# Feed-forward on one core: gate and up as one row of 1408 columns over three PSUM banks

## The reference, cut to what matters

```python
BLOCK = 16
def fp4_quant_dequant(x):                      # last dim in blocks of 16
    xb = x.reshape(shape[:-1] + (shape[-1] // BLOCK, BLOCK))
    scale = jnp.max(jnp.abs(xb), axis=-1, keepdims=True) / 6.0
    scale = jnp.maximum(scale, jnp.float32(1e-12))
    xn = xb / scale
    idx = jnp.searchsorted(_MID, jnp.abs(xn))
    q = _GRID[idx] * jnp.sign(xn) * scale
    return q.reshape(shape)

def fp4_linear(x, w):
    return jnp.einsum('bsk,nk->bsn', fp4_quant_dequant(x), fp4_quant_dequant(w))

gate = fp4_linear(x, w_gate)                   # 256 -> 704
y = fp4_linear(x, w_up)                        # 256 -> 704
h = jax.nn.silu(gate) * y
return fp4_linear(h, w_down)                   # 704 -> 256
...
x = x + _L0_attn_a_ref(_layernorm(x), ...)
x = x + _L0_ffn_ref(_layernorm(x), w_gate, w_up, w_down)
x = x + _L0_attn_b_ref(_layernorm(x), ...)
x = x + _L0_ffn_ref(_layernorm(x), w_gate, w_up, w_down)
```

## Time and profile before

| | |
|---|---|
| median of 3 runs | 3568.77 us (3567.9 to 3569.11) |
| span of the profiled execution, first to last instruction | 3544.7 us |
| PE busy | 3052.4 us, 86% of the span |
| DVE busy | 2796.0 us, 79% |
| ACT busy | 2188.0 us, 62% |
| POOL busy | 1119.2 us, 32% |

### The profile page before, as it was taken

One profiled execution on the slowest core, in us unless ns is written; L12 is line 12 of the kernel. 1 busy time (PEld: TensorE's weight loads), 2 busy tenths in 40 slices (PEclk: granted clock), 3 DMA queues, 4 the chain that ended last, 5 costly groups with the idle time before them and its releaser, 6 DMA issues. The chain is left out here.

```text
span 3544.7 us, 69866 instructions
## 1 busy us (share of the span) xinstructions
PE 3052.4 (86%) x23640; PEld 2351.6 (66%) x23640; DVE 2796.0 (79%) x7241; ACT 2188.0 (62%) x5392; POOL 1119.2 (32%) x665
## 2 busy tenths in 40 slices
PE   5898888988886999995888888888888886799998
PEld 3666666666655888884555556556555554788888
DVE  4777777767767999992788888888888886799997
ACT  3777777777762434441777878777777785344443
POOL 1000000000004555553124444433333343455554
PEclk9999999999996999997899989999999997899999
DMA  5354453534422000001344444344434443111000
GB/s 91 51 75 65 61 76 50 75 65 62 72 37 106 13 19 19 19 19 30 48 63 69 64 73 69 60 63 70 66 60 70 68 61 83 42 37 34 28 31 25
DMA packets 134180, 193.96 MB, mean 55 GB/s; under 512 B 15126, under 2 KB 81558, under 8 KB 133142
## 3 DMA queue, kind: packets, MB, share of 16 engines
q1 hardware_dynamic: 133830, 189.49, 31.3%
HBM read 45.65 MB, written 28.84 MB: 21 GB/s over the span
## 5 line engine op out<-in xcount | busy, mean ns | idle before, releaser
L436 ACT ACTIVATE a_probs<-a_probs,a_negmax 128x176 f32<-128x176 f32 (+4 forms) x1024 | 502.4, 491 | 261.0 <-DVE a_negmax L355 257.2
L355 DVE CUSTOM_DVE_ANT_0 a_probs<-a_mask,a_score 128x176 f32<-128x176 f32 (+4 forms) x1024 | 403.6, 399 | 254.5 <-PE a_score L511 116.6
L520 PE MATMUL a_turned<-ident,a_probs 128*128 128x128 f32 (+1 forms) x2176 | 405.2, 280 | 60.3 <-DVE a_pT L364 32.8
L1752 DVE CUSTOM_DVE_ANT_0 b_u<-b_u,b_score 128x512 f32<-128x512 f32 x512 | 340.3, 680 | 129.7 <-PE b_score L2007 128.3
L1877 ACT ACTIVATE b_u<-b_u,b_negmax 128x512 f32<-128x512 f32 x512 | 367.1, 717 | 107.0 <-DVE b_negmax L1752 105.4
L1281 PE MATMUL f_y_bank<-f_wdT,f_hqT 128*128 128x256 f32 x1536 | 357.0, 382 | 40.7 <-ACT f_hqT L1220 37.7
L1744 DVE SCALAR_TENSOR_TENSOR b_u<-b_u,b_score 128x1024 f32<-128x1024 f32 x256 | 309.6, 1214 | 92.1 <-ACT b_u L1870 89.6
L1870 ACT ACTIVATE b_u<-b_score 128x1024 f32<-128x1024 f32 x256 | 262.2, 1025 | 159.8 <-PE b_score L1997 159.3
L1281 PEld LDWEIGHTS f_y_bank<-f_wdT,f_hqT 128*128 128x128 f32 x1536 | 284.6, 190 | 89.6 <-issue 56.5
L2016 PE MATMUL b_turned<-ident,b_u 128*128 128x128 f32 x2048 | 318.1, 280 | 24.1 <-DVE b_pT L1758 18.9
L520 PEld LDWEIGHTS a_turned<-ident,a_probs 128*128 128x128 f32 (+1 forms) x2176 | 237.3, 134 | 136.1 <-ACT a_probs L436 61.5
(11 more groups left out here) (237 smaller groups left out, 7037.0 us busy)
## 6 DMA issues: line engine op xcount, KB each, us to landing
b_stack<-b_part SPq DMA_DIRECT2D x192, 256.0 KB, 8.1
a_stack_q<-a_part SPq DMA_DIRECT2D x192, 128.0 KB, 4.5
a_wide_k<-a_part SPq DMA_DIRECT2D x96, 164.0 KB, 7.8
a_stack_k<-a_part SPq DMA_DIRECT2D x96, 128.0 KB, 4.6
xs<-in_x_dram SPq DMA_DIRECT2D x16, 512.0 KB, 10.6
x_before_b<-xs SPq DMA_DIRECT2D x16, 512.0 KB, 2.9
b_xin<-x_before_b SPq DMA_DIRECT2D x16, 512.0 KB, 12.3
b_xres<-x_before_b SPq DMA_DIRECT2D x16, 512.0 KB, 3.8
```

Source lines behind the costliest of these rows:

```text
L355: dve.tensor_tensor_reduce(out=probs[:, n % 2, j, 0:keys(n)], in0=mask_of(n), in1=score[j][:, 0:keys(n)], scale=-1.0, scalar=3.0e38, op0=A ...
L436: act.activation(probs[:, n % 2, j, 0:keys(n)], probs[:, n % 2, j, 0:keys(n)], ACT.Exp, bias=negmax[:, n, j:j + 1], scale=-1.0, accum_out= ...
L520: m = nc.tensor.transpose(turned[j % 2][0:rows, u, :], chunk(n, probs[:, n % 2, j, :], u), ident[:])
L1752: dve.tensor_tensor_reduce(out=u[:, n, j, :], in0=u[:, n, j, :], in1=score[:, j, :], scale=-0.05, scalar=3.0e38, op0=ALU.add, op1=ALU.min, ...
```

## The change

Gate and up get one tensor of three banks, gate_up, in place of two of two banks each. The weights of both already stand side by side as 1408 columns; they are now cut at the banks' borders into 512, 512 and 384 columns in place of four pieces of 352. Each piece is still six products, so a tile has 18 in place of 24. Gate is columns 0 to 703, up is 704 to 1407: bank 1 holds the end of gate and the beginning of up. s_gate is raised by the last product of bank 1, s_up by that of bank 2. Bank 0 waits for the silu of the tile before, banks 1 and 2 wait for its f_hid. The bank that comes free holds the block maxima (`amax`, two tiles of 44 columns), which lay in SBUF; in the profile of the changed kernel they have the name f_scaled.

```diff
-        amax = sb("amax", [P, 2, NB])
...
-        gate = pb("gate", [P, 2, SEQ])
-        up = pb("up", [P, 2, SEQ])
+        gate_up = pb("gate_up", [P, 3 * SEQ])
         xT_bank = pb("xT_bank", [P, SEQ])
         hT_bank = pb("hT_bank", [P, 2 * SEQ])
+        scaled = pb("scaled", [P, SEQ])
         y_bank = pb("y_bank", [P, SEQ])
+        amax = [scaled[:, i * NB:(i + 1) * NB] for i in range(2)]
...
                 dve.wait_ge(s_silu, T + 1)
                 dve.wait_ge(s_up, T + 1)
-                dve.tensor_tensor(out=hid[:, i, :].rearrange("p (a b) -> p a b", a=2),
-                                  in0=silu[:, i, :].rearrange("p (a b) -> p a b", a=2),
-                                  in1=up[:, :, both], op=ALU.mult).then_inc(s_hid, 1)
+                dve.tensor_tensor(out=hid[:, i, :], in0=silu[:, i, :], in1=gate_up[:, INNER:2 * INNER],
+                                  op=ALU.mult).then_inc(s_hid, 1)
                 dve.wait_ge(s_hid, T + 1)
-                dve.tensor_reduce(out=amax[:, i, :], in_=blocks(hid[:, i, :]), axis=AX.X, op=ALU.max,
+                dve.tensor_reduce(out=amax[i], in_=blocks(hid[:, i, :]), axis=AX.X, op=ALU.max,
                                   apply_absolute_value=True).then_inc(s_h, 1)
                 dve.wait_ge(s_h, 2 * T + 1)
-                dve.tensor_scalar(out=nscale[:, t, :], in0=amax[:, i, :], scalar1=-SIXTH, scalar2=-SCALE_MIN,
+                dve.tensor_scalar(out=nscale[:, t, :], in0=amax[i], scalar1=-SIXTH, scalar2=-SCALE_MIN,
                                   op0=ALU.mult, op1=ALU.min)
-                dve.tensor_scalar(out=amax[:, i, :], in0=amax[:, i, :], scalar1=SIXTH * TIE_DOWN, scalar2=SCALE_MIN,
+                dve.tensor_scalar(out=amax[i], in0=amax[i], scalar1=SIXTH * TIE_DOWN, scalar2=SCALE_MIN,
                                   op0=ALU.mult, op1=ALU.max).then_inc(s_h, 1)
                 dve.wait_ge(s_h, 2 * T + 2)
-                dve.reciprocal(out=inv[:, i, :], in_=amax[:, i, :]).then_inc(s_inv, 1)
+                dve.reciprocal(out=inv[:, i, :], in_=amax[i]).then_inc(s_inv, 1)
...
                 act.wait_ge(s_gate, T + 1)
-                act.activation(silu[:, t % 2, :].rearrange("p (a b) -> p a b", a=2), gate[:, :, 0:HALF],
-                               ACT.Silu).then_inc(s_silu, 1)
+                act.activation(silu[:, t % 2, :], gate_up[:, 0:INNER], ACT.Silu).then_inc(s_silu, 1)
...
-            def expand(s, t, which):
+            def expand(s, t, bank):
+
                 T = tile(s, t)
-                if which == 0:
+                if bank == 0:
                     pe.wait_ge(s_xTm, 4 * s + t + 1)
-                free = (s_silu, s_hid)[which]
-                wait(pe, free, T)
-                dst = (gate, up)[which]
-                for a in range(2):
-                    at = which * INNER + a * HALF
-                    products = [(k, i, j) for k in range(KC) for i, j in ((0, 0), (0, 1), (1, 0))]
-                    for p, (k, i, j) in enumerate(products):
-                        m = mm(dst[:, a, 0:HALF], xqT[:, i, k, t * P:(t + 1) * P], wguT[:, j, k, at:at + HALF],
-                               start=p == 0, stop=p == len(products) - 1)
-                m.then_inc((s_gate, s_up)[which], 1)
+                wait(pe, (s_silu, s_hid, s_hid)[bank], T)
+                at = slice(bank * SEQ, min((bank + 1) * SEQ, 2 * INNER))
+                products = [(k, i, j) for k in range(KC) for i, j in ((0, 0), (0, 1), (1, 0))]
+                for p, (k, i, j) in enumerate(products):
+                    m = mm(gate_up[:, at], xqT[:, i, k, t * P:(t + 1) * P], wguT[:, j, k, at],
+                           start=p == 0, stop=p == len(products) - 1)
+                if bank:
+                    m.then_inc((s_gate, s_up)[bank - 1], 1)
...
                     if t is not None:
                         expand(s, t, 1)
+                        expand(s, t, 2)
                     if behind(3):
                         down(*behind(3))
```

More of the change, by code:

```diff
@@ L975, in ffn @@
     NB = INNER // BLOCK
-    HALF = INNER // 2
     LAG = 3
@@ L1133, in hidden @@
                 T, i = tile(s, t), t % 2
-                both = slice(0, HALF)
                 if not isinstance(T, int) or T >= 2:
```

## The result

| | before | after |
|---|---|---|
| median, same chip | 3568.94 us (3567.9 to 3569.12, 4 runs) | 3609.06 us (3608.42 to 3615.59, 4 runs) |
| ratio, 95% interval | | 1.0126 (1.0112 to 1.0140) |
| span of the profiled execution | 3544.7 us | 3607.3 us |

The account below looks back on a forecast made before the run. DVE's chain bounds the kernel (31.15 us per four tiles), TensorE close behind; at 8.09 us per tile, two stages add 42 us: span 3544.7 to 3587, plus 24.1 around it, gives 3610 us, range 3570 to 3635.

Parts of the forecast that it names:

- The chain bank 1, silu, move, down product: TensorE and ScalarE: 1.87 us needed against bank 2's 1.05, so a 0.82 us wait before every down product.
- Fewer products: TensorE's gate and up: 18 products in place of 24 save 0.02 us per tile, range 0 to 0.12.
- The period: Feed-forward time per tile: 7.29 + 0.82 - 0.02 = 8.09 us.
- f_nscale: DVE scaling of 44 columns: PSUM input cuts 0.84 to about 0.17 us; net gain for the kernel taken as 0.
- f_hid at even distances: Sign in the profile after: f_hid, gate times up, stands 8.1 us apart in all four slots.
- the part on bank 1: Bank 1's wait for the previous tile's f_hid stays hidden; cover gone only if DVE fell 4.6 us behind.
- the three signs of being wrong: f_y_bank waiting under 0.5 us, f_hid at unequal distances again, or the 18 products clearly under 3.9 us.
- What lies around the span: Time outside the profiled span: 3568.77 - 3544.7 = 24.1 us, added to the forecast span of 3587.
- The range: Forecast's own range 3592 to 3628 us; widened to 3570 to 3635 to hold 8 in 10.
- The faster rival: ScalarE's move arrives in time, DVE sets 29.8 us per sequence: -40 us, 3529; needs wait below 0.50 us; chance 0.15.
- The draw: Wait before the down product is 0.45 to 0.55 us, giving 3562 to 3575 us; chance 0.05.
- the slower rival: Dear PSUM operations on DVE or a falling granted clock add 15 to 30 us: 3625 to 3640; chance 0.05.

Follow-up runs that it names:

- the move first: Changed kernel with ScalarE's move of f_hT_bank to f_hqT (tile T-3) put before the silu of tile T; 3526.69 us, ratio to before 0.9901.
- transposes between: Changed kernel with TensorE's six transposes of f_hq put between bank 1 and bank 2, ScalarE's order kept; 3537.17 us, ratio to before 0.9945.
- Both magnitudes swapped: Changed kernel with move before silu and, in slot 0, magnitude of h before that of x; profiled twice; 3505.75 us, again 3503.92 us.

## Why the prediction was right, point by point

- *The chain bank 1, silu, move, down product:* shown. Taken away it gives 85 us back (the move first), covered by other work it gives 72 (transposes between), lengthened by 0.65 us it costs 78, and put into the old kernel it costs 66 to 69. The wait was forecast at 0.82 us by start times; it is 3.33 less 2.53 of products, 0.80. The profile counts 127 such waits in the 128 tiles of both stages and shows it here as 0.64, since it counts from the products' modelled end.
- *Fewer products:* 0.02 us was forecast. It is nothing: where TensorE does not wait (the timeline under "Both magnitudes swapped"), bank 0 takes 1.47 us and banks 1 and 2 take 2.53, 4.00 us as in the earlier trace rows. The cost went with the 8448 columns. The other end, 0.12 us, is excluded, and so is a period under 8 us.
- *The period:* 8.17 for 8.09 us. Two terms were mis-sized: the 0.02 above, and a down product that follows a wait takes 2.66 us, not 2.59. The earlier trace rows had that in them (in the same timeline the next instruction starts 2.67 us later), and I had read the 2.59 from a product without a wait. The 120 intervals grew by 50.5 us where 42 was forecast, and the first slots of the stages by 1.6, which were to stay: 52.
- *f_nscale:* 0.20 us for the expected 0.17, gain 0.63 for 0.67, and all of it swallowed, as forecast, by the residual's wait; the other small operations cost 0.01 to 0.03 us more each (f_amax 895 for 886 ns, the second scaling 202 for 173, the reciprocal 433 for 428). The 0.3 us that I had allowed each did not come.
- *f_hid at even distances:* wrong, 8.16, 8.17, 9.78 and 6.55. Slot 1 still has GpSimd's f_xq in it, DVE falls 1.6 us behind and catches up in slot 2, as the part on bank 1 had it; the line on what would show it forgot this. It was also one of the three signs of being wrong, and by itself it would have condemned a mechanism that held. The other two, a wait under 0.5 us and products under 3.9 us, did not appear. TensorE's period was even.
- *What lies around the span:* this step was wrong. The prediction took 24.1 us, the median less the span of one profiled execution. Where a run's own span is given with its time, the difference is 1.7 to 1.8 us (3609.04 against 3607.3). So the execution profiled before took some 3546 us, 22 less than the median of the runs. The span of 3607.3 is 3544.7, the 52 of the stages, 10.6 of the second attention block (1428.2 us in place of 1417.6, with the same code) and small ends. The forecast of the span, 3587, was thus 20 us short, half of it in the stages and half in a block that was taken as fixed, and the 24.1 us added behind it were 22 too many. That the total came out within 1 us is luck. By the medians the rise is 40 us and by the stages 52; no profile tells where the median execution of before spent the difference.
- *The range:* 12 us either way for the wait and up to 12 less for the products would give 3586 to 3622. The 3592 to 3628 in the text do not follow from its terms; the measured time lies in both.
- *The faster rival* failed at its condition, a wait under 0.50 us. Its chain was right: with the wait gone DVE takes 29.89 us per sequence (29.8 forecast). Its price was near: the stages are 33 us under before and the median 27, where 40 was forecast. The period of 29.8 also needed a wait under (29.8 - 29.16) / 4 = 0.16 us, which the text does not say: with one of 0.16 to 0.50 TensorE sets a period in between, as the 30.3 us of the transposes between the banks. The draw and the slower rival did not occur; the granted clock stayed 1.00 in the slots with waits.

## What to carry to other kernels

When a value becomes ready one piece later, follow the in-order queue of the engine that uses it: what stands behind the user there is late too, and here that was an older tile's move for which TensorE itself waited. Add the durations from the late semaphore to the next wait of the bounding engine and set them against the work that it has left in between; 1.87 against 1.05 us decided this case. And a faster operation counts only after the waits behind it are looked at: the maxima in PSUM were worth nothing in one order and some 40 us in the other.

## What the runs showed of the hardware that was not expected

- A DVE scaling of 44 columns that reads SBUF took 837 ns on average while a GpSimd multiplication ran and ended with it; reading PSUM and writing SBUF it took 203, every time within 1 ns in the stage's middle. The Trainium skill ("SBUF — State Buffer", Who interferes with whom) says so of operations in a two-port mode, and the trace agrees. The marks with two SBUF inputs still waited in the new kernel (2.51 us). The second scaling, SBUF to SBUF, took 0.17 us in most tiles and 1.98 when it started with GpSimd's f_xu: it is a matter of when it starts, and one kernel can have it in some sequences and not in others.
- float32r products cost by the column, 0.455 ns (512 columns every 0.233 us, 384 every 0.175, 352 every 0.160), above 1/2.4 = 0.417 ns at a granted clock of 1.00. What makes the difference no run here tells.
- The kernel before took 3542 to 3568 us in 16 executions on one chip, at mean granted clocks of 0.950 down to 0.937. Of the version profiled twice, the 60 intervals of a stage repeated within 0.02 us, while whole stages differed by up to 2.4 us, in their first slots. The second attention block, whose code is the same in all kernels, took from 1417.6 to 1433.2 us in the profiled executions, at a granted clock of 0.90 in the six where it took up to 1426.4 us and 0.88 or 0.89 in the five where it took 1428.2 or more. Differences of 10 us are read from the stage, not from the total. What decides the block's clock in one execution was not tried.
